# Attention probabilities of the second graph layer: split before they are turned, and turned by DMA instead of TensorE

## The reference

```python
def _sparse_attention(x, src, dst, wq, bq, wk, bk, wv, bv, wo, bo):
    q = (x @ wq + bq).reshape(N, H, Dh) * Dh ** (-0.5)
    k = (x @ wk + bk).reshape(N, H, Dh)
    v = (x @ wv + bv).reshape(N, H, Dh)
    scores = jnp.einsum('ehd,ehd->eh', q[src], k[dst])
    smax = jax.ops.segment_max(scores, src, num_segments=N)
    ex = jnp.exp(scores - smax[src])
    denom = jax.ops.segment_sum(ex, src, num_segments=N)
    attn = ex / denom[src]
    out = jax.ops.segment_sum(attn[:, :, None] * v[dst], src, num_segments=N)
    return out.reshape(N, D) @ wo + bo
```

## Time and profile before

| What | us |
|---|---|
| median of three runs | 2639.08 (2635.67 to 2639.22) |
| the profiled execution, its own time | 2643.26 |
| its span, first to last instruction | 2641.5 |
| PE busy in the span | 2334.9 |
| DVE busy | 1705.2 |
| ACT busy | 1028.4 |
| POOL busy | 746.5 |

### The profile page before, as it was taken

The page is one execution under the profiler, slowest core; times in us unless marked ns, Lnnn a source line. Parts: engine busy times, 40 slices in busy tenths (PEclk is TensorE's granted clock), DMA queues, the critical chain, the costliest instruction groups (busy, mean ns, idle before and its releaser), DMA issues. The chain is left out here.

```text
span 2641.5 us, 37845 instructions
## 1 busy us (share of the span) xinstructions
PE 2334.9 (88%) x14014; PEld 1768.4 (67%) x14014; DVE 1705.2 (65%) x3208; ACT 1028.4 (39%) x1782; POOL 746.5 (28%) x627
## 2 busy tenths in 40 slices
PE   6889979999899999999999899999895988888873
PEld 6884458888778888777888777888772543333331
DVE  8995265666665667655666554666645045899985
ACT  1113045445434545334555344545420031334342
POOL 0000042212542121642120553121520000566673
PEclk9999989999999999999999999999997998889886
DMA  1011220001120000210000211000227000000001
GB/s 64 31 41 45 81 77 9 9 9 51 51 65 9 9 9 21 72 56 22 9 12 20 61 53 33 9 12 22 64 97 178 12 19 1 0 0 0 1 0 39
DMA packets 68306, 90.78 MB, mean 34 GB/s; under 512 B 21237, under 2 KB 37621, under 8 KB 68129
## 3 DMA queue, kind: packets, MB, share of 16 engines
q1 hardware_dynamic: 68129, 88.41, 11.3%
HBM read 62.94 MB, written 25.45 MB: 33 GB/s over the span
## 5 line engine op out<-in xcount | busy, mean ns | idle before, releaser
L1035 POOL TENSOR_SCALAR inverse_mass_diagonal<-identity,row_masses 125x125 f32<-125x125 f32 x160 | 96.7, 605 | 790.4 <-DVE row_masses L826 623.0
L1358 ACT ACTIVATE urned_probabilities_high<-psum 125x500 bf16<-125x500 f32 (+1 forms) x480 | 214.7, 522 | 249.2 <-PE psum L1203 249.2
L1520 DVE TENSOR_TENSOR turned_probabilities_low<-psum,urned_probabilities_high 125x500 bf16<-125x500 f32 (+1 forms) x480 | 253.6, 585 | 73.4 <-ACT urned_probabilities_high L1358 72.8
L814 DVE CUSTOM_DVE_ANT_0 probabilities<-psum,counts 125x1250 f32<-125x1250 f32 x160 | 233.5, 1459 | 104.3 <-PE psum L664 67.0
L1850 POOL TENSOR_TENSOR logs_and_shifts<-logs_by_source,target_spreads 125x1250 f32<-125x1250 f32 x80 | 216.1, 2704 | 156.8 <-DVE probabilities_turned L1923 94.3
L2069 PE MATMUL psum<-probabilities_turned,values_and_ones 125*65 125x512 f32 (+1 forms) x480 | 210.7, 585 | 39.3 <-ACT probabilities_turned L1986 21.5
L1361 ACT ACTIVATE probabilities<-probabilities,row_peaks 125x1250 f32<-125x1250 f32 x160 | 216.0, 1350 | 56.4 <-DVE row_peaks L818 55.2
L662 PE MATMUL psum<-urned_probabilities_high,values_high 125*128 125x250 bf16 x800 | 217.6, 272 | 10.7 <-DVE attended_turned L1482 6.5
L664 PE MATMUL psum<-urned_probabilities_high,values_low 125*128 125x250 bf16 x800 | 215.0, 269 | 0.0
L663 PE MATMUL psum<-turned_probabilities_low,values_high 125*128 125x250 bf16 x800 | 214.7, 268 | 0.0
L1923 DVE SCALAR_TENSOR_TENSOR probabilities_turned<-target_spreads,source_bends,logs_and_shifts 125x1250 f32<-125x1250 f32 x80 | 203.2, 2546 | 15.5 <-POOL logs_and_shifts L1850 15.5
(11 more groups left out here) (271 smaller groups left out, 5385.9 us busy)
## 6 DMA issues: line engine op xcount, KB each, us to landing
weight_stage<-in_L_gnn_m_w SPq DMA_DIRECT2D x32, 256.0 KB, 2.6
block_inputs_kept<-nodes SPq DMA_DIRECT2D x8, 896.0 KB
counts_kept<-counts_by_target_rows SPq DMA_DIRECT2D x10, 625.0 KB, 3.4
counts_by_target<-counts_kept SPq DMA_DIRECT2D x1, 6103.5 KB
logs_kept<-counts SPq DMA_DIRECT2D x1, 5468.8 KB
nodes<-block_inputs_kept SPq DMA_DIRECT2D x12, 448.0 KB
logs_by_source<-logs_kept SPq DMA_DIRECT2D x1, 4375.0 KB
weight_stage<-in_L_gnn_wv SPq DMA_DIRECT2D x16, 256.0 KB, 2.6
```

The costliest lines, as they stand in the source:

```text
L814: dve.tensor_tensor_reduce(prob[0:TILE, i % 2, :], scores, fx.count_src[0:TILE, i, 0:NODES], scale, MASKED, ALU.add, ALU.max, p[:, 0:1]).t ...
L1358: nc.scalar.activation(dst, src, ACT.Copy).then_inc(pt_high, 1)
L1520: dve.tensor_tensor(dst, src, high, ALU.subtract).then_inc(pt_low, 1)
```

## The change

In the attention stage the probabilities are first scaled by the inverse mass and split, on their own rows: ACT writes the high part with the mass as scale (`high_part`), DVE the low part (`low_part`), both in bf16 into `parts` (2 buffers x 20 blocks x 128). One DMA from SP (`dma_start_transpose`) turns all twenty blocks into `pt`, again two buffers. `weighted` takes one row tile at a time, ten blocks x three matmuls of 125 columns, into bank 6 or 7, three steps after its scores (LAG); its result needs no scaling and is copied by ACT (`attend`). Gone are PE's transposes and mass products, ACT's and DVE's three splits of the turned exponentials, DVE's scaling of the pair and POOL's diagonals. The scores have two PSUM regions in turn (`score_bank`), so `scores` waits for the read of two steps ago. Of the next head's six projections four stay behind the tenth step, and two move behind the next head's first scores. POOL clears `parts` once a block. On SP the loads of weights for later heads now stand between the transfers. `attended_low` and `last_attended_low` work tile by tile in the last head. The rest of the diff renumbers semaphores to match.

```diff
-        pt_h = place("turned_probabilities_high", [128, 2, TILES, 250], BF16)
-        pt_l = place("turned_probabilities_low", [128, 2, TILES, 250], BF16)
-        mass_rows = place("inverse_mass_rows", [128, 2, 250], F32)
-        mass_diag = place("inverse_mass_diagonal", [128, 2, TILE], F32)
+        pt = place("turned_probability_parts", [128, 2, 2 * TILES, 128], BF16)
+        parts = packer(nc, WORK_AT + TILES * DIM * 4)("probability_parts", [128, 2, 2 * TILES, 128], BF16)
...
+        PROJECTIONS = ((0, 0), (1, 0), (1, 1), (1, 2), (0, 1), (0, 2))
         PROJ_CUTS = ((0, 500), (500, 1000), (1000, NODES))
         CUT_TILES = (4, 8, TILES)
+        STEPS, LAG = TILES * HEADS1, 3
...
+        def score_bank(h, i):
+            return 3 * ((h + i) % 2)
+        def projection_bank(h, c):
+            return (3, 7)[c % 2] if h == 0 else score_bank(h, 1) + c % 3
...
+                for h in range(HEADS1):
+                    for i in range(TILES):
+                        T = 40 * b + 10 * h + i
+                        sp.wait_ge(part_low, T + 1)
+                        if T >= 2:
+                            sp.wait_ge(pv_done, T - 1)
+                        sp.dma_start_transpose(pt[:, T % 2], parts[:, T % 2].rearrange("p d n -> p (d n)")).then_inc(turned[T % 2], 16)
+                        if h < HEADS1 - 2 and i in (5, 8):
+                            k = 8 + 2 * h + (i == 8)
+                            weight(b, k, head_of((wq, wk)[k % 2], b, h + 2))
+                        if h == HEADS1 - 2 and i in (5, 8):
+                            weight(b, 12 + (i == 8), rows_of(wo, b, int(i == 8)))
+                        if h == 0 and i == 2:
+                            condition(b, ((s2, sb2), (t2, tb2)), 1)
+                        if h == HEADS1 - 1 and i == 3:
+                            sp.wait_ge(proj_prod, 24 * b + 24)
+                            sp.wait_ge(x_spilled, 96 * b + 96)
+                            for a, z in ROW_PARTS:
+                                sp.dma_start(early[a:z], kept[a:z, 0:EARLY]).then_inc(x_early, 16)
...
+                pool.memset(parts[96:128], 0.0).then_inc(parts_clear, 1)
+                pool.wait_ge(parts_clear, 2 * b + 1)
+                pool.memset(parts[:, :, :, TILE:128], 0.0).then_inc(parts_clear, 1)
...
                 def scores(h, i):
                     T = 40 * b + 10 * h + i
-                    if h > 0 or i > 0:
+                    if i == 0 and h > 0:
                         pe.wait_ge(scored, T)
+                        pe.wait_ge(proj_low, 24 * b + 6 * h + 4)
+                    elif i == 1 and h > 0:
+                        pe.wait_ge(proj_low, 24 * b + 6 * h + 6)
+                    elif i >= 2:
+                        pe.wait_ge(scored, T - 1)
...
+                def weighted(h, i):
+                    T = 40 * b + 10 * h + i
+                    pe.wait_ge(turned[T % 2], 16 * (T // 2 + 1))
+                    if T >= 2:
+                        pe.wait_ge(o_done, T - 1)
+                    for d in range(TILES):
+                        mm = three(pe, bank(6 + T % 2)[:, 0:TILE], [p[0:TILE, d, h * HDIM1:(h + 1) * HDIM1] for p in (v_h, v_l)],
+                                   [pt[0:TILE, T % 2, k * TILES + d, 0:TILE] for k in range(2)], d == 0, d == TILES - 1)
+                    mm.then_inc(pv_done, 1)
...
+                    for i in range(TILES):
+                        scores(h, i)
+                        if i >= LAG:
+                            weighted(h, i - LAG)
                         if i == 0 and h > 0:
+                            weighted(h - 1, TILES - 2)
+                            project(b, h, (4, 5))
                             weighted(h - 1, TILES - 1)
+                    if h < HEADS1 - 1:
+                        project(b, h + 1, (0, 1, 2, 3))
+                        weighted(h, TILES - 3)
                     else:
+                        for i in range(TILES - LAG, TILES):
+                            weighted(h, i)
+                pe.wait_ge(scored, 40 * b + 40)
+                pe.wait_ge(o_done, 40 * b + 40)
...
+                def exponentials(h, i):
+                    T = 40 * b + 10 * h + i
+                    act.wait_ge(peaked, T + 1)
+                    nc.scalar.activation(prob[0:TILE, T % 2, :], prob[0:TILE, T % 2, :], ACT.Exp,
+                                         bias=fx.peak[0:TILE, T % 2, 1:2],
+                                         accum_out=fx.mass[0:TILE, i, 0:1]).then_inc(exped, 1)
+                def high_part(h, i):
+                    T = 40 * b + 10 * h + i
+                    act.wait_ge(inverted, T + 1)
+                    if T >= 2:
+                        act.wait_ge(turned[T % 2], 16 * (T // 2))
+                    nc.scalar.activation(parts[0:TILE, T % 2, 0:TILES, 0:TILE], by_tile(prob[0:TILE, T % 2, :]), ACT.Copy,
+                                         scale=fx.mass[0:TILE, i, 2:3]).then_inc(part_high, 1)
+                def attend(h, i):
+                    T = 40 * b + 10 * h + i
+                    act.wait_ge(pv_done, T + 1)
+                    if h < HEADS1 - 1:
+                        nc.scalar.activation(attended[:, h, cols(i)], bank(6 + T % 2)[:, 0:TILE], ACT.Copy).then_inc(o_done, 1)
+                    else:
+                        nc.scalar.activation(y_h[:, h, cols(i)], bank(6 + T % 2)[:, 0:TILE], ACT.Copy).then_inc(att_high, 1)
...
+                    for i in range(TILES):
+                        if i >= 1:
+                            high_part(h, i - 1)
+                        exponentials(h, i)
+                        if i >= LAG:
+                            attend(h, i - LAG)
+                        if i == 0 and h > 0:
+                            attend(h - 1, TILES - 2)
+                            projected_high(b, h, (4, 5))
+                            attend(h - 1, TILES - 1)
+                        if not more and i < HEADS1 - 1:
+                            attended_high(i)
+                    high_part(h, TILES - 1)
                     if more:
+                        projected_high(b, h + 1, (0, 1, 2, 3))
+                        attend(h, TILES - 3)
+                    else:
+                        output_weights_high(12)
+                        output_weights_high(13)
+                        attend(h, TILES - 3)
+                        attend(h, TILES - 2)
+                        output_weights_high(14)
+                        output_weights_high(15)
+                        attend(h, TILES - 1)
...
+                def low_part(h, i):
+                    T = 40 * b + 10 * h + i
+                    dve.wait_ge(part_high, T + 1)
+                    dve.scalar_tensor_tensor(parts[0:TILE, T % 2, TILES:2 * TILES, 0:TILE], by_tile(prob[0:TILE, T % 2, :]),
+                                             fx.mass[0:TILE, i, 2:3], parts[0:TILE, T % 2, 0:TILES, 0:TILE],
+                                             ALU.mult, ALU.subtract).then_inc(part_low, 1)
                 for h in range(HEADS1):
                     more = h < HEADS1 - 1
+                    for i in range(TILES):
                         T = 40 * b + 10 * h + i
+                        if i >= 1:
                             row_mass(dve, i - 1, T - 1)
+                        wait_apart(dve, fx, qk_done, T + 1)
+                        if T >= 2:
+                            dve.wait_ge(part_low, T - 1)
+                        at = BANK * score_bank(h, i)
+                        row_scores(dve, psum[0:TILE, at:at + NODES], i, T, HDIM1 ** -0.5)
                         if i == 0 and h > 0:
+                            projected_low(b, h, (4, 5))
+                        if i >= 1:
+                            low_part(h, i - 1)
+                        if not more and 1 <= i <= HEADS1 - 1:
+                            attended_low(i - 1)
+                        if not more and i > LAG:
+                            last_attended_low(i - LAG - 1)
+                    row_mass(dve, TILES - 1, T)
                     if more:
+                        projected_low(b, h + 1, (0,))
+                    low_part(h, TILES - 1)
+                    if more:
+                        projected_low(b, h + 1, (1, 2, 3))
                     else:
+                        for i in range(TILES - LAG - 1, TILES):
+                            last_attended_low(i)
```

## The result

| | before | after |
|---|---|---|
| median, 20 runs each | 2638.6 us | 2652.1 us |
| ratio of after to before | | 1.0047, 95% interval 1.0036 to 1.0058 |
| profiled execution, its span | 2643.3, 2641.5 | 2648.3, 2646.4 |
| mean granted clock of TensorE | 0.95 | 0.92 |

The sign is wrong; the time lies inside the range of 2520 to 2790. PE lost 141 us of work, and before the change it was busy 61.7 of the 63.1 us of a head, yet the kernel gained nothing; so the question is where they went.

The account below looks back on a forecast made before the run. PE, busy 88%, bounded the kernel; afterwards covering a 5.0 us landing would set 4.03 us steps. A block takes 212.5 against 229.6 us, four blocks -68: 2643.3 becomes 2575, less 4.2 for the median, 2571 us; range 2520 to 2790.

Parts of the forecast that it names:

- 3P >= D + 7.1: Attention steps: three steps of P us must cover a transfer's landing D plus 7.1 us of other work.
- D = 5.0 gives P = 4.03: Attention steps: a landing of 5.0 us, the middle of 3.4 and 6.6, makes each step 4.03 us.
- The likeliest case of the prediction: Attention stage: landing of 4 to 6.5 us, kernel faster at 2571 us, own range 2544 to 2631; chance 0.40.
- what would make it wrong: Heads: among the signs against the forecast, PE's granted clock falling because PE idles, which nothing in it pays for.
- nothing that is due: SP queue: weight loads, two in a head, 2.6 to 3.1 us to landing, stall nothing that is due.
- 20 times the 0.20 us: Block start: POOL's clearing of the parts priced as 20 times the 0.20 us of L152.
- beside the first scores, at most 0.5 uncovered: Block start: POOL's clearing falls beside the first scores, at most 0.5 us of it uncovered.
- The third rival: Weighted products on PE: weight loads show through, 78 ns a product, 2.34 us a row tile, 2612 us; chance 0.05.
- The chain: DVE and ACT in one step: score read, exponential and its sum, maximum, reciprocal and waits sum to 3.75 us.
- a clean passage: Between heads: from the last score read to the next head's second read, 24.5 us by PE's new order.
- The rival of a slow transfer: SP transfer: slower kernel from 6.7 us landing or 4.6 us in the queue; 2777 us at 10 us; chance 0.35.
- the fourth rival: SP transfer: landing near 6.7 us, tail and waits take back the steps' gain, time within 0.2%; chance 0.05.

Follow-up runs that it names:

- Keep busy: Changed kernel with 72 extra 125-column products on TensorE at each head's start, before its wait for the turned parts: 2647.7 us, ratio 1.0030 to the kernel before.
- three buffers: Changed kernel with three buffers in place of two for parts and turned parts, one plane of attended values kept: 2646.1 us, ratio 1.0027 to the kernel before.
- plain copy: Changed kernel with each step's turned transfer replaced by a plain copy of the same bytes: 2563.1 us, ratio 0.9707 to the kernel before.
- two halves: Changed kernel with each step's transfer cut in two, the scaled high half leaving before the low one: 2587.8 us, ratio 0.9812 to the kernel before.
- lag 4: Changed kernel with three buffers for parts and turned parts, and weighted values four steps behind in place of three: 2583.0 us, ratio 0.9791 to the kernel before.
- first early: Changed kernel with mass, high and low part of row 0 of heads 1 to 3 ahead of the last two projections: 2646.4 us, ratio 1.0024.

## Why the prediction was wrong

**The step that failed** is the condition 3P >= D + 7.1, from which "D = 5.0 gives P = 4.03" followed, used as if every landing were the same and PE as fast behind a wait as ahead of it. The forecast thought of steps of 4.0 throughout. What came is 3.5, 3.5 and then a stall. That alone would cost nothing: 3.5, 3.5 and 5.1 have the same mean. But behind a wait of 4.5 us in one piece the granted clock was 0.50, and 6.66 came in place of 5.1. The likeliest case of the prediction was the right mechanism in its parts, but not in its balance: eight steps took 34.3 us in heads 1 and 2 where 32.2 were forecast, and the whole margin was 17 us a block. The parts below are estimates from the rows; they are no sum, since the experiments show that what one of them gives back the next wait takes:

- **The granted clock.** The prediction named it as what would make it wrong and put no price on it. Behind a wait of 4.5 us the weighted product takes 3.1 us at a granted clock of 0.50, in place of 1.65 at 1.00. With the undisturbed cost the fifth read would come 11.6 us behind the second, better than D + 7.1 = 12.1; it came 13.7 behind. Keep busy shows 1.8 us a head where the landing stays 4.8, which would be 1.8 x 12 = 22 us for heads 0 to 2 of the four blocks; taken away by itself it gained nothing that the times show. The tail pays too: 17.9 in place of 13.8.
- **One landing for all.** The median was right (4.9 against 5.0), the mean is 5.36, and a wait is set by the long ones. By the prediction's own condition 5.36 gives P = 4.15, 33 x 0.12 x 4 = 15 us. With three buffers and TensorE kept busy at lag 3 the steps come at 4.2, close to what the condition gives for the 5.39 that its landings have on the mean, 4.16; the condition's 1.8 us for a product that took 1.65 and the clock of 0.98 pull in opposite ways there, so the agreement is in part luck.
- **The early rows.** The prediction let SP's other loads stall "nothing that is due" and did not name these. The transfer behind them lands in 7.8 to 9.3 us, row 8 of the last head takes 9.34 us, 5.3 more than the 4.03 of the forecast: 21 us in four blocks. The longer landing behind them was read from the trace and not tested by moving them.
- **POOL's clearing.** Its size was nearly right ("20 times the 0.20 us" is 4.0, measured 4.6), its cover was not: "beside the first scores, at most 0.5 uncovered" left out that it starts behind POOL's last low values, at 414.55, while the exponential is due about 417.2. The first step takes 6.97 in place of 4.03: 2.9 a block, 12 us. Moving the wait took 2.1 of it off the first gap, and the rows behind took most of that again.
- **The loop over the two buffers of parts.** Not in the prediction, which looked only at those of the turned parts. ACT's scaled part of row T waits for the landing of T-2, 129.8 us in all. Shown not to matter by itself (three buffers). That it is one of the things that give back what is won elsewhere (rows 5 to 8 of keep busy) is not shown: with three buffers and TensorE kept busy together these rows take 17.0 us in place of 17.9, and the buffers' own gain there is 0.2.

**What was right.** Thirty products of 125 columns start 55 ns apart, 1.65 us a row, where 59 ns and 1.8 were taken from the edge products. The third rival, dearer products, did not come true. The chain runs at 3.5 where 3.75 was taken, 2,560 pieces of 256 B were counted rightly, and a clean passage is 24.3 (plain copy) against 24.5. The rival of a slow transfer did not hold either: 3.08 us in the queue and 4.9 to landing stay under its limits of 4.6 and 6.7, and yet its sign came out. Nor was there the landing near 6.7 of the fourth rival, which had the time unchanged within 0.2%. So it is luck that 2652 lies in the range: its upper part was there for a slow transfer, and that is not what happened. Between the forecast's two ends for the landing, 3.4 and 6.6 us, the turned transfer came near the middle: about 215 GB/s against the plain one's about 400, and 4.9 us against 3.4 to landing. The plain copy shows what that difference is worth, 89 us, with the shorter hold of the queue.

**What the experiments settle.** Lag 3 with a landing of 4.9 is short of cover: either a shorter landing (plain copy, two halves) or one more step (lag 4) takes most of the stalls away, and of what was tried nothing else does. That it is the cover, and not the time that a transfer holds the queue, is shown by lag 4, where the transfers are as they were. Taking away a single stall (first early) moves it a row on; taking away the fall of the clock (keep busy) or the buffer (three buffers) leaves it or has it made up for by other rows. **What stays open**: that long landings are caused by TensorE's code loads rests on the order of events in the changed kernel and on counts in several. No experiment confirms it, since neither kernel made to raise these loads did so by more than 5 packets in 116.

## What to carry to other kernels

When work is moved from a busy engine to a transfer that it then waits for, price the wait twice: the time itself (here 4.5 us), and what the engine does at a lower clock behind it (here 3.1 us in place of 1.65 at a granted clock of 0.50). A condition of the form "so many steps cover the landing" should hold for the long landings of a queue (here 27 of 160 over 6.2 us), not for the median (4.9); if it holds with less than a step to spare, plan one more step of lag or cut the transfer so that its first part leaves earlier. Each of the two was worth over 60 us here, and both together, with a third buffer for the turned parts, turned a loss of 0.5% into a gain of 3%. And look at what else stands in the queue: the transfers issued behind the early rows' 1,000 KB landed in 7.8 to 9.3 us in place of 4.9.

## What the runs showed of the hardware

- A turned transfer between two places in SBUF of 128 x 2,560 two-byte values holds SP's queue 3.08 us and lands in 4.9; half of it 1.37 and 3.6; the plain copy 0.46 and 3.4.
- Turned transfers that coincide with a 16 KB packet of instruction loads landed in 5.94 us on the mean, others in 5.07; 21 of 22 whose packet started 4.4 to 4.7 us behind their issue landed 1.0 to 1.2 us behind the packet's end.
- A turned transfer issued behind 1,000 KB of loads in the same queue landed in 7.8 to 9.3 us.
- Behind 4.5 us without a product the granted clock was 0.50 of full speed, and thirty products of 125 columns took 3.1 us in place of 1.65.
- POOL's clearing of 32 partitions x 5,120 two-byte values took 4.36 us.
- TensorE's 144 waits on a semaphore that had long reached its value took 5.9 us of PE's time at most heads' starts, up to 6.2, so these passed waits were not free on PE: some 40 ns each.
